# Attention scores in half legs: maxima turned per four heads and 256 queries, a score bank with two heads of one row half, lead of 14 maximum tiles

## The chip, the cores and the metric

The kernel is one launch on one core of a Trainium2 chip. The metric is the device time of that launch in microseconds (us). Five engines run their own instruction streams and meet at semaphores: PE (TensorE, the matmuls), DVE (VectorE), ACT (ScalarE), POOL (GpSimd) and SP (SyncE, which only issues DMAs here).

## The reference

Two transformer-like blocks run one after the other over 2 x 1024 tokens of 128 channels. The change touches only the attention of the first block:

```python
h = _layernorm(x, axis=-1) * (1 + ca) + sa
def _L0_attn_ref(x, Wq, Wk, Wv):
    H, hd = 16, 8
    q = (x @ Wq.T).reshape(N, S, H, hd).transpose(0, 2, 1, 3)
    k = (x @ Wk.T).reshape(N, S, H, hd).transpose(0, 2, 1, 3)
    v = (x @ Wv.T).reshape(N, S, H, hd).transpose(0, 2, 1, 3)
    energy = jnp.einsum('nhqd,nhkd->nhqk', q, k)
    attn = jax.nn.softmax(energy / jnp.sqrt(jnp.float32(hd)), axis=3)
    out = jnp.einsum('nhql,nhld->nhqd', attn, v)
    return out.transpose(0, 2, 1, 3).reshape(N, S, D)
x = x + ga * attention(h)
```

Behind it come the coupling network, two Mamba layers and a mixture of experts, all untouched by the change. With 2 sequences and 16 heads there are 32 heads, each with 1024 queries and 1024 keys.

## The kernel before, in words

**Tiling.** Queries and keys lie in bf16 rows, each number split into three bf16 parts, so that 48 rows (`KR`) carry the product of 8 channels, and 3 more rows (up to `KM` = 51) carry the negated maximum of each query. Of two neighbouring heads one lies in partitions 0 to 50, the other in 64 to 114 (`head_rows`: `64 * (j % 2)`), called row half 0 and row half 64 here. A *leg* is four heads and 512 queries; there are 16 legs. The heads of a leg are j = 0 to 3; j = 0 and 2 are in row half 0, j = 1 and 3 in row half 64.

**Three kinds of work.** (m) A *maximum tile* is 128 queries of one head against 1024 keys: two matmuls of 512 columns (`pe_max_score`, L548) into `max_ps`, which has room for two tiles, then one DVE reduction over 1024 columns (`ve_max_score`, L559). A leg has 16 tiles, the whole attention 256. When a leg's 16 tiles are reduced, POOL splits the maxima into three bf16 parts (`po_max_parts`, L568 to L574), PE turns them (`pe_max_turn`, L590), ACT copies them out (L596) and SP puts them into the query rows with four DMAs (`sp_max_turn`, L603). This is a *turn*. (s) A *score bank* is one matmul of 51 rows, 128 keys by 512 queries of one head (`pe_score`, L667), and one ACT exponential of 512 columns (`ac_exp`, L675). `HEADS` gives the order of the heads: (1, 3, 0, 2). A leg has 32 score banks. Three PSUM banks (`score_k`) go round (`score_bank`) among scores, turns and results: a new user waits for ACT to have read what was three users ago. (v) The product with the values is four matmuls of 256 columns over all 128 partitions (`pe_av`, L694), two for each group of four score banks; each shows in the profile as two records.

**Order.** The order is written out by hand. `ahead(v)` puts the first `AHEAD` = 22 maximum tiles ahead of all scores; the turn of leg 0 stands behind the tile `NU + 2` = 18. Then come 65 rounds of four tiles, eight score banks and four v each, by the strings in `ROUNDS`:

```python
ROUNDS = ("msmsvmsmsvvmsmsvmsms", "msmsmsmsvmsmsvvmsmsv", "msmsvmsmsvmsmsvmsmsv", "msmsvmsmsvmsmsvmsmsv")
return ((0, 2, 1, 3)[k // 4], k % 4) if leg == 0 else (k // 8 * 2 + k % 2, k % 8 // 2)
HEADS = (1, 3, 0, 2)
s, row = head_rows(leg, HEADS[r % 4])
```

Each `m` is one of a tile's two matmuls, so `msms` is one tile and two score banks; I call it a *slot*. PE takes its stream in this order. By `tile_of` the tiles alternate between row half 0 and row half 64 from slot to slot, and by `HEADS` the score banks are two of half 64 and then two of half 0. The strings have `v` behind most slots, and once in a leg three slots follow each other with no `v` between (the end of place 0 and the start of place 1). The turn of the next leg stands at the end of place 2, the loads of later heads (`sp_load`) behind it on SP. When the tiles are through, the last 22 slots have scores and values alone; DVE then does the first steps of the next stage (`ve_first_batch`).

Of the kernel before, what the change touches and what calls it, by code (L numbers as in the profile page):

```python
# [22 lines left out]
P = 128  # L23
# [5 lines left out]
TB = S // P  # L29
# [117 lines left out]
class Kernel:  # L147
# [282 lines left out]
    def attention(self):  # L430
        nc, A, pe, ve, ac, po, sp = self.nc, self.A, self.pe, self.ve, self.ac, self.po, self.sp
        with ExitStack() as scope:
# [16 lines left out]
            nr = sb("neg_max_rest", [P, 4, 4])  # L449
            ms = [sb(f"neg_max_parts{s}", [P, 4, 3, 4], BF16) for s in range(2)]  # L450
            mt = [sb(f"neg_max_rows{s}", [48, P], BF16) for s in range(2)]
# [69 lines left out]
            NLEG, NU, AHEAD = BH // 2, 16, 22  # L521
# [11 lines left out]
            def tile_of(leg, k):  # L533


                return ((0, 2, 1, 3)[k // 4], k % 4) if leg == 0 else (k // 8 * 2 + k % 2, k % 8 // 2)

            def pe_max_score(leg, k, half):
                t = NU * leg + k
                j, qt = tile_of(leg, k)  # L540
                s, row = head_rows(leg, j)
                if half == 0:
                    if t == 0:
                        pe.wait_ge(*first_half.at())
                    elif k == (0 if leg else 8):
                        pe.wait_ge(*loaded_at[leg // 2])
                    wait_from(pe, max_read.sem, t - 1)
# [5 lines left out]
            def ve_max_score(leg, k):  # L553
                j, qt = tile_of(leg, k)
                bank = (NU * leg + k) % 2 * 2
                if k == 0:
                    wait_from(ve, split.sem, 4 * (leg - 1))
                ve.wait_ge(*max_mm.at())
                ve.tensor_reduce(nm[leg % 2][:, 4 * j + qt:4 * j + qt + 1],  # L559
# [3 lines left out]
            def po_max_parts(leg):  # L563

                z, o = nm[leg % 2][:].rearrange("p (h k) -> p h k", h=4), ms[leg % 2]
                po.wait_ge(*max_read.at())
                wait_from(po, max_turned.sem, leg - 1)
# [8 lines left out]
            def max_score(v):  # L576

                leg, k, half = v // 2 // NU, v // 2 % NU, v % 2
                if leg >= NLEG:
                    return  # L580
                pe_max_score(leg, k, half)
                if half:
                    ve_max_score(leg, k)
                    if k == NU - 1:
                        po_max_parts(leg)

            def pe_max_turn(leg, bank, free):
                pe.wait_ge(split.sem, 4 * leg + 4)
                wait_from(pe, *free)
                pe.transpose(eps[:, bank, 0:64].bitcast(BF16)[0:3 * NU, :],  # L590
                             ms[leg % 2][:].rearrange("p h a k -> p (h a k)"), self.identb[:]).then_inc(*max_turned.up())

            def ac_max_turn(leg, bank):
                ac.wait_ge(max_turned.sem, leg + 1)
                wait_from(ac, max_in[leg % 2].sem, 64 * (leg // 2))
                ac.activation(mt[leg % 2][:], eps[:, bank, 0:64].bitcast(BF16)[0:3 * NU, :], ACT.Copy).then_inc(  # L596
                    *turn_read.up())

            def sp_max_turn(leg):
                sp.wait_ge(turn_read.sem, leg + 1)  # L600
                for j in range(4):
                    s, row = head_rows(leg, j)
                    sp.dma_start(qp[row + KR:row + KM, s, leg % 2, :].rearrange("a (k q) -> a k q", k=4),  # L603
                                 mt[leg % 2][12 * j:12 * j + 12, :]).then_inc(*max_in[leg % 2].up(16))
# [28 lines left out]
            def max_turn(leg):  # L633

                bank, free = score_bank()
                pe_max_turn(leg, bank, free)
                ac_max_turn(leg, bank)
                sp_max_turn(leg)
# [19 lines left out]
            HEADS = (1, 3, 0, 2)  # L658

            def pe_score(leg, r, bank, free):  # L660
# [2435 lines left out]
```

## Time and profile before

| what | us |
|---|---|
| median of 3 runs | 1158.91 |
| the three runs | 1160.96, 1148.05, 1158.91 |
| the profiled execution's own time | 1150.8 |
| its span, first to last instruction | 1149.3 |
| attention in it, to PE's first matmul of the next stage (L397) | 378.71 |

All sums below are made in the profiled execution, whose own time is 1.5 us over its span. It is not the middle of the runs: the median is 8 us longer. PE is the busiest engine by the page (90% of the span), DVE the next (84%).

### The profile page before, as it was taken

To read this page: it belongs to the slowest core of one execution; us is meant where nothing else is said; L and a number is where in the kernel's file an instruction comes from. 1 tells how busy PE (TensorE), PEld (TensorE's weight loads), DVE (VectorE), ACT (ScalarE), POOL (GpSimd) and SP (SyncE) were. 2 spreads that over 40 slices of the span, in tenths; PEclk is the share of its full clock that TensorE was granted. 3 is DMA by queue.
4 is the path that set the end of the run, shared out by engine and by line. 5 is a ranking of instruction groups with operands and counts; after the bars stand their busy time and mean duration, and the time that the engine had idled before them with its cause. 6 is when DMAs were issued, how large, how long until landed. Compare 5 with 4: busy or idle time off the path is not lost. (4 is left out here: it accounts for less than half of the span.)

```text
span 1149.3 us, 21244 instructions
## 1 busy us (share of the span) xinstructions
PE 1036.9 (90%) x7771; PEld 648.5 (56%) x7771; DVE 968.1 (84%) x1309; ACT 814.9 (71%) x1621; POOL 520.9 (45%) x487
## 2 busy tenths in 40 slices
PE   6899999999999887889999999899999984699992
PEld 4222222222222334458998984468888964488992
DVE  6899999999995676979999996989999996767774
ACT  3279898999998644978888844888888922265561
POOL 5400431010101211027899991048999972256663
PEclk9779999999999988799999999899999995699996
DMA  5210100001000420107999980118999967311124
GB/s 158 69 43 15 30 16 21 25 16 30 15 2 2 130 56 2 58 2 178 244 248 224 223 205 3 58 43 193 234 242 224 242 144 253 41 43 41 43 48 121
DMA packets 58374, 114.40 MB, mean 100 GB/s; under 512 B 15406, under 2 KB 28718, under 8 KB 58272
## 3 DMA queue, kind: packets, MB, share of 16 engines
q0 software_dynamic: 14880, 50.23, 22.2%
q1 hardware_dynamic: 40152, 60.62, 16.8%
q10 hardware_dynamic: 3240, 2.20, 0.7%
q8 instruction: 62, 1.02, 0.4%
q14 instruction: 40, 0.33, 0.1%
HBM read 55.47 MB, written 9.13 MB: 56 GB/s over the span
## 5 line engine op out<-in xcount | busy, mean ns | idle before, releaser
L2245 PEld LDWEIGHTS m_pair<-filter_w,delta_x_t 128*128 128x128 f32 x2560 | 294.0, 192 | 43.1 <-issue 43.1
L559 DVE TENSOR_REDUCE neg_max<-max_ps 128x1 f32<-128x1024 f32 x256 | 295.6, 1214 | 15.2 <-PE max_ps L548 15.0
L2245 PE MATMUL m_pair<-filter_w,delta_x_t 128*128 128x112 f32 (+3 forms) x2560 | 298.5, 276 | 9.8 <-DVE h_t L2272 3.3
L675 ACT ACTIVATE exp_scores<-score_k 128x512 f32<-128x512 f32 x512 | 270.8, 605 | 28.4 <-PE score_k L667 22.7
L2221 ACT ACTIVATE decay<-delta,a_log 128x1024 f32<-128x1024 f32 x128 | 145.7, 1142 | 49.7 <-DVE normed L2272 29.7
L548 PE MATMUL max_ps<-k_rows,q_rows 48*128 48x512 bf16 x512 | 163.0, 400 | 12.4 <-DVE neg_max L559 10.7
L2213 ACT ACTIVATE filter_w<-filter,b_t 128x112 f32<-128x112 f32 (+1 forms) x576 | 167.4, 374 | 0.0
L667 PE MATMUL score_k<-q_rows,k_rows 51*128 51x512 bf16 x512 | 163.0, 389 | 2.4 <-ACT exp_scores L675 0.6
L694 PE MATMUL av_ps<-exp_scores,v_cols 128*32 128x256 f32 x2048 | 158.2, 394 | 0.0
L568 POOL CAST neg_max_parts<-neg_max 128x16 bf16<-128x16 f32 x16 | 3.2, 197 | 235.0 <-DVE neg_max L559 235.0
L694 PEld LDWEIGHTS av_ps<-exp_scores,v_cols 128*32 128x32 f32 x2048 | 44.2, 109 | 92.0 <-ACT exp_scores L675 52.8
L548 PEld LDWEIGHTS max_ps<-k_rows,q_rows 48*128 48x128 bf16 x512 | 29.4, 95 | 116.4 <-DVE neg_max L559 75.0
L2263 DVE TENSOR_TENSOR_SCAN m_pair<-decay,m_pair 128x1024 f32<-128x1024 f32 x38 | 87.0, 2289 | 1.6 <-PE m_pair L2245 1.2
L2310 POOL TENSOR_TENSOR h_t<-h_t,c_row 128x1024 f32<-128x1024 f32 x30 | 81.6, 2718 | 13.0 <-DVE h_t L2272 13.0
L2310 POOL TENSOR_TENSOR normed<-normed,c_row 128x1024 f32<-128x1024 f32 x28 | 76.0, 2714 | 23.4 <-DVE normed L2272 23.4
L2907 PE MATMUL gate_up_ps<-tile_t,gate_up 128*128 128x128 f32 x624 | 77.6, 278 | 3.0 <-DVE tile_t L2889 2.0
L2272 DVE TENSOR_TENSOR_SCAN normed<-decay,m_pair 128x1024 f32<-128x1024 f32 x32 | 73.0, 2280 | 8.7 <-PE m_pair L2245 8.7
L2272 DVE TENSOR_TENSOR_SCAN h_t<-decay,m_pair 128x1024 f32<-128x1024 f32 x32 | 73.0, 2280 | 6.0 <-PE m_pair L2245 6.0
L2907 PEld LDWEIGHTS gate_up_ps<-tile_t,gate_up 128*128 128x128 f32 x624 | 72.7, 192 | 6.8 <-DVE tile_t L2889 6.8
L2358 PE MATMUL m_pair<-delta_x,ident 128*128 128x512 f32 x136 | 68.3, 598 | 0.0
L2920 ACT ACTIVATE silu_gate<-gate 128x512 f32<-128x512 f32 x39 | 24.6, 630 | 46.9 <-DVE gate L2915 46.9
L2946 POOL DMA_INDIRECT moe_out_rows<-tile_out,row_to x39 | 38.9, 996 | 38.6 <-ACT tile_out L2941 37.7
(335 smaller groups left out, 1631.4 us busy)
## 6 DMA issues: line engine op xcount, KB each, us to landing
c_row<-c_rows SPq DMA_DIRECT2D x64, 512.0 KB, 6.0
x_inner<-normed POOLq DMA_DIRECT2D x16, 512.0 KB, 6.5
delta_x<-mod_memory POOLq DMA_DIRECT2D x15, 512.0 KB, 8.1
delta_x<-x_inner POOLq DMA_DIRECT2D x15, 512.0 KB, 8.3
x_inner<-h_t POOLq DMA_DIRECT2D x14, 512.0 KB, 5.7
mod_memory<-h_t POOLq DMA_DIRECT2D x14, 512.0 KB, 9.2
mod_memory<-normed POOLq DMA_DIRECT2D x12, 512.0 KB, 8.8
gate_up_all<-in_gate_up_w SPq DMA_DIRECT2D x8, 512.0 KB, 7.3
```

The source lines that it names most:

```text
L548: mm = pe.matmul(mps[:, t % 2 * 2 + half, :], qp[row:row + KR, s, leg % 2, qt * P:(qt + 1) * P], kp[row:row + KR, s, half * CH:(half + 1) ...
L559: ve.tensor_reduce(nm[leg % 2][:, 4 * j + qt:4 * j + qt + 1], mps[:, bank:bank + 2, :].rearrange("p a q -> p (a q)"), AX_X, ALU.max, negat ...
L667: pe.matmul(eps[:, bank, :], kp[row:row + KM, s, kt * P:(kt + 1) * P], qp[row:row + KM, s, leg % 2, :], start=True, stop=True).then_inc(*s ...
L675: ac.activation(pt[a % 4][:, HEADS[r % 4], :], eps[:, bank, :], ACT.Exp, scale=SC).then_inc(*exped.up())
L694: mm = pe.matmul(avp[32 * j:32 * j + 32, qs], va[quad % 2][:, j, kt, :], pt[a % 4][:, j, qs], start=(kt == half == 0), stop=(kt == TB - 1) ...
L2213: w = ac.activation(wf[g % 3][:, lo:c * STEP + P], tri[min(c, 1)][:], ACT.Copy, scale=self.bT[b][:, c, n:n + 1])
L2221: ac.activation(da[u % 4], delta[:, blk, b, :], ACT.Exp, scale=am[:, l, blk, n:n + 1]).then_inc(*decay.up())
L2245: mm = pe.matmul(vps[blk][:, lo:hi], self.duT[b][:, c, blk * P:(blk + 1) * P], wf[g % 3][:, lo:hi], start=True, stop=True)
L2263: ve.tensor_tensor_scan(to, da[u % 4], vps[0][:], 0.0, ALU.mult, ALU.add).then_inc(*hs.up())
L2272: ve.tensor_tensor_scan(hh[g % 4], da[u % 4], vps[1][:], 0.0, ALU.mult, ALU.add).then_inc(*hs.up())
L2310: po.tensor_tensor(yacc[b][1] if n == 1 else hh[g % 4], hh[g % 4], csb[g % 3][:], ALU.mult).then_inc(*yg.up())
L2907: mm = pe.matmul(gups[j % 2][:, half, f * P:(f + 1) * P], gu[j % 3][:, half * FF + f * P:half * FF + (f + 1) * P], xt[j % 2][:], start=Tru ...
```

## The change

A turn now covers four heads and 256 queries (8 tiles, `NU` = 8), so there are 32 turns (`NTURN`) in place of 16, each with half the data: 24 rows in place of 48, DMAs of half the size. A score bank now holds two heads of 256 queries, both of one row half: two matmuls of 256 columns in place of one of 512. The exponential still takes 512 columns. `HEADS` is indexed by `r % 2`: banks alternate between half 64 (heads 1, 3) and half 0 (heads 0, 2). `ROUNDS` is as it was, and so is the alternation of the tiles' halves from slot to slot. `AHEAD` is 14. The turn of turn 0 stands behind tile 10, those that follow at the end of places 0 and 2. The memsets `po_ones(2, NS)` on POOL move from behind the projections to behind the split of turn 0, and SP's first loads wait for them. `ve_first_batch` takes two steps where it took one.

```diff
-            NLEG, NU, AHEAD = BH // 2, 16, 22
+            NLEG, NU, AHEAD = BH // 2, 8, 14
+            NTURN, HQ = 2 * NLEG, CH // 2
-                return ((0, 2, 1, 3)[k // 4], k % 4) if leg == 0 else (k // 8 * 2 + k % 2, k % 8 // 2)
+                j, q = ((0, 2, 1, 3)[k // 2], k % 2) if turn == 0 else (k // 4 * 2 + k % 2, k % 4 // 2)
+                return j, turn % 2 * 2 + q
...
-            HEADS = (1, 3, 0, 2)
+            HEADS = ((1, 3), (0, 2))
-                kt = r // 4
-                s, row = head_rows(leg, HEADS[r % 4])
+                leg, q0, kt = turn // 2, turn % 2 * HQ, r // 2
                 if r == 0:
-                    pe.wait_ge(max_in[leg % 2].sem, 64 * (leg // 2 + 1))
+                    pe.wait_ge(max_in[turn % 2].sem, 64 * (turn // 2 + 1))
                 wait_from(pe, *free)
-                pe.matmul(eps[:, bank, :], kp[row:row + KM, s, kt * P:(kt + 1) * P], qp[row:row + KM, s, leg % 2, :],
-                          start=True, stop=True).then_inc(*score_mm.up())
+                for c, j in enumerate(HEADS[r % 2]):
+                    s, row = head_rows(leg, j)
+                    mm = pe.matmul(eps[:, bank, c * HQ:(c + 1) * HQ], kp[row:row + KM, s, kt * P:(kt + 1) * P],
+                                   qp[row:row + KM, s, leg % 2, q0:q0 + HQ], start=True, stop=True)
+                mm.then_inc(*score_mm.up())
...
-                pe.wait_ge(exped.sem, 4 * a + 4)
+                pe.wait_ge(exped.sem, 4 * a + kt % 2 * 2 + 2)
...
                     max_turn(0)
+                    po.wait_ge(*split.at())
+                    po_ones(2, NS)
+                    sp.wait_ge(*rows_set.at())
                     for half in range(2):
                         sp_load(1, half)
...
-                po.wait_ge(*part_lo.at())
-                po_ones(2, NS)
-                sp.wait_ge(*rows_set.at())
...
                         if v % 2 == 0:
-                            ve_first_batch(v // 2 - NLEG * NU - 1)
+                            for step in range(2):
+                                ve_first_batch(v - 2 * NTURN * NU - 2 + step)
...
+                if place % 2 == 0 and n // 2 + 1 < NTURN:
+                    max_turn(n // 2 + 1)
                 if place == 2 and leg + 1 < NLEG:
-                    max_turn(leg + 1)
```

On PE in the middle of the attention, a slot with its v and the start of the next slot stood so before (`max_ps` is the tile, `score_k` the score bank, `av_ps` the product with the values):

```order
L548 MATMUL max_ps<-k_rows,q_rows 128x512
L667 MATMUL score_k<-q_rows,k_rows 128x512
L548 MATMUL max_ps<-k_rows,q_rows 128x512
L667 MATMUL score_k<-q_rows,k_rows 128x512
L694 MATMUL av_ps<-exp_scores,v_cols 32x256 x4
L548 MATMUL max_ps<-k_rows,q_rows 128x512
L667 MATMUL score_k<-q_rows,k_rows 128x512
```

and it stands so now:

```order
L550 MATMUL max_ps<-k_rows,q_rows 128x512
L673 MATMUL score_k<-q_rows,k_rows 128x256 x2
L550 MATMUL max_ps<-k_rows,q_rows 128x512
L673 MATMUL score_k<-q_rows,k_rows 128x256 x2
L702 MATMUL av_ps<-exp_scores,v_cols 32x256 x4
L550 MATMUL max_ps<-k_rows,q_rows 128x512
L673 MATMUL score_k<-q_rows,k_rows 128x256 x2
```

The order of kinds is the same; what changed is that each score bank is two matmuls, and the row half in which each bank lies.

The second place is PE at the end of place 0, inside the run of three slots without v. Nothing stood between the slots before; now the turn of a half leg does (L593 is `pe_max_turn`):

```order
L702 MATMUL av_ps<-exp_scores,v_cols 32x256 x4
L550 MATMUL max_ps<-k_rows,q_rows 128x512
L673 MATMUL score_k<-q_rows,k_rows 128x256 x2
L550 MATMUL max_ps<-k_rows,q_rows 128x512
L673 MATMUL score_k<-q_rows,k_rows 128x256 x2
L593 MATMUL score_k<-identb,neg_max_parts 24x128
L550 MATMUL max_ps<-k_rows,q_rows 128x512
L673 MATMUL score_k<-q_rows,k_rows 128x256 x2
L550 MATMUL max_ps<-k_rows,q_rows 128x512
```

So each leg has one more transpose on PE, which takes a score bank of its own.

The third place is POOL at the start, from the last split of the projections on. Before, the memset of the key rows came ahead of the first split of maxima:

```order
L788 TENSOR_TENSOR part<-part_rest,part 128x512 x4
L467 MEMSET k_rows 32x4096 x2
L568 CAST neg_max_parts<-neg_max 128x4x4
L570 TENSOR_TENSOR neg_max_rest<-neg_max,neg_max_parts 128x16
L572 CAST neg_max_parts<-neg_max_rest 128x4x4
L574 TENSOR_TENSOR neg_max_parts<-neg_max_rest,neg_max_parts 128x4x4
L655 COPY v_cols<-v_tok 128x8x8 x4
```

Now it stands behind it:

```order
L800 TENSOR_TENSOR part<-part_rest,part 128x512 x4
L571 CAST neg_max_parts<-neg_max 128x4x2
L573 TENSOR_TENSOR neg_max_rest<-neg_max,neg_max_parts 128x8
L575 CAST neg_max_parts<-neg_max_rest 128x4x2
L577 TENSOR_TENSOR neg_max_parts<-neg_max_rest,neg_max_parts 128x4x2
L467 MEMSET k_rows 32x4096 x2
L660 COPY v_cols<-v_tok 128x8x8 x4
```

The split of turn 0 has moved ahead of the memset, and the copy of the first values stays behind it.

## Rows read from the trace of the kernel before

**Rows 1.** Groups of the page: line engine op, busy us, mean ns, idle before

```profile
L559 DVE TENSOR_REDUCE neg_max<-max_ps 128x1 f32<-128x1024 f32 x256 | 295.6, 1214 | 15.2 <-PE max_ps L548 15.0
L675 ACT ACTIVATE exp_scores<-score_k 128x512 f32<-128x512 f32 x512 | 270.8, 605 | 28.4 <-PE score_k L667 22.7
L667 PE MATMUL score_k<-q_rows,k_rows 51*128 51x512 bf16 x512 | 163.0, 389 | 2.4 <-ACT exp_scores L675 0.6
```

**Rows 2.** Windows: PE, PEld, DVE, ACT, POOL busy (count), PEclk, DMA share, GB/s

```profile
66.00:70.00 4.00, 3.82 (x24) 0.66 (x24) 3.25 (x4) 2.93 (x6) 0.00 (x0) 0.50 0.13 42
...
240.00:300.00 60.00, 58.95 (x615) 17.33 (x617) 57.12 (x54) 55.38 (x109) 5.15 (x23) 1.00 0.09 25
```

**Rows 3.** Timeline of PE, two slots and a turn: start us, us, instruction

```profile
212.07 0.39 PE L548 MATMUL max_ps<-k_rows,q_rows 48*128 48x512 bf16 x1
212.07 0.39 PE L667 MATMUL score_k<-q_rows,k_rows 51*128 51x512 bf16 x1
212.30 0.38 PE L548 MATMUL max_ps<-k_rows,q_rows 48*128 48x512 bf16 x1
...
212.61 0.64 PE L694 MATMUL av_ps<-exp_scores,v_cols 128*32 128x256 f32 x8
213.18 0.39 PE L548 MATMUL max_ps<-k_rows,q_rows 48*128 48x512 bf16 x1
...
215.39 0.24 PE L590 MATMUL score_k<-identb,neg_max_parts 128*48 128x128 bf16 x1
215.56 0.39 PE L548 MATMUL max_ps<-k_rows,q_rows 48*128 48x512 bf16 x1
```

**Rows 4.** Timeline of PE: ends of one leg, and the run of three slots

```profile
205.18 0.39 PE L548 MATMUL max_ps<-k_rows,q_rows 48*128 48x512 bf16 x1 [0.21 <-DVE neg_max L559]
...
223.82 0.39 PE L548 MATMUL max_ps<-k_rows,q_rows 48*128 48x512 bf16 x1
...
224.63 0.39 PE L548 MATMUL max_ps<-k_rows,q_rows 48*128 48x512 bf16 x1 [0.21 <-DVE neg_max L559]
...
226.62 0.64 PE L694 MATMUL av_ps<-exp_scores,v_cols 128*32 128x256 f32 x8
```

**Rows 5.** Timeline of PE: matmuls of one row half behind each other

```profile
38.28 1.03 PE L548 MATMUL max_ps<-k_rows,q_rows 48*128 48x512 bf16 x4
...
352.93 0.60 PE L667 MATMUL score_k<-q_rows,k_rows 51*128 51x512 bf16 x2
353.46 0.64 PE L694 MATMUL av_ps<-exp_scores,v_cols 128*32 128x256 f32 x8
```

**Rows 6.** Timeline: weight loads between f32 matmuls of 512 columns, and 16 of 128

```profile
16.40 0.19 PEld L764 LDWEIGHTS score_k<-h_t,w_qkv 128*128 128x128 f32 x1 [0.24 <-issue]
16.83 0.19 PEld L764 LDWEIGHTS score_k<-h_t,w_qkv 128*128 128x128 f32 x1 [0.24 <-issue]
...
36.40 1.95 PE L801 MATMUL score_k<-w_qkv,h_t 128*128 128x128 f32 x16
```

**Rows 7.** Timeline of the lead: reductions, memset, first turn, first score

```profile
38.92 22.39 DVE L559 TENSOR_REDUCE neg_max<-max_ps 128x1 f32<-128x1024 f32 x19 [0.42 <-PE max_ps L548]
...
40.96 7.06 POOL L467 MEMSET k_rows<- 32x4096 bf16 x2
...
54.28 0.20 POOL L568 CAST neg_max_parts<-neg_max 128x16 bf16<-128x16 f32 x1 [6.25 <-DVE neg_max L559]
...
57.11 3.14 SPq L603 DMA_DIRECT2D q_rows<-neg_max_rows  x4
...
61.36 0.60 PE L667 MATMUL score_k<-q_rows,k_rows 51*128 51x512 bf16 x1 [0.58 <-DMA q_rows<-neg_max_rows]
```

**Rows 8.** Timeline of the slots without tiles, to the next stage

```profile
349.38 0.60 PE L667 MATMUL score_k<-q_rows,k_rows 51*128 51x512 bf16 x2
...
368.75 8.63 ACT L675 ACTIVATE exp_scores<-score_k 128x512 f32<-128x512 f32 x16
...
378.71 0.42 PEld L397 LDWEIGHTS max_ps<-ident,normed 128*128 128x128 f32 x4 [0.41 <-issue]
```

More of the change, by code:

```diff
@@ L531, in head_rows, with tile_of, pe_max_score @@
                 return 2 * (leg // 2 % 3) + j // 2, 64 * (j % 2)
-            def tile_of(leg, k):
-                return ((0, 2, 1, 3)[k // 4], k % 4) if leg == 0 else (k // 8 * 2 + k % 2, k % 8 // 2)
-            def pe_max_score(leg, k, half):
-                t = NU * leg + k
-                j, qt = tile_of(leg, k)
+            def tile_of(turn, k):
+                j, q = ((0, 2, 1, 3)[k // 2], k % 2) if turn == 0 else (k // 4 * 2 + k % 2, k % 4 // 2)
+                return j, turn % 2 * 2 + q
+            def pe_max_score(turn, k, half):
+                t, leg = NU * turn + k, turn // 2
+                j, qt = tile_of(turn, k)
                 s, row = head_rows(leg, j)
@@ L544, in pe_max_score @@
                         pe.wait_ge(*first_half.at())
-                    elif k == (0 if leg else 8):
+                    elif k == (0 if turn else 4) and turn % 2 == 0:
                         pe.wait_ge(*loaded_at[leg // 2])
@@ L576, in max_score @@
             def max_score(v):
-                leg, k, half = v // 2 // NU, v // 2 % NU, v % 2
-                if leg >= NLEG:
+                turn, k, half = v // 2 // NU, v // 2 % NU, v % 2
+                if turn >= NTURN:
                     return
-                pe_max_score(leg, k, half)
+                pe_max_score(turn, k, half)
                 if half:
-                    ve_max_score(leg, k)
+                    ve_max_score(turn, k)
                     if k == NU - 1:
-                        po_max_parts(leg)
@@ L587, in pe_max_turn @@
-            def pe_max_turn(leg, bank, free):
-                pe.wait_ge(split.sem, 4 * leg + 4)
+                        po_max_parts(turn)
+            def pe_max_turn(turn, bank, free):
+                pe.wait_ge(split.sem, 4 * turn + 4)
                 wait_from(pe, *free)
                 pe.transpose(eps[:, bank, 0:64].bitcast(BF16)[0:3 * NU, :],
[L591 to L596, printed above, removed]
+                             ms[turn % 2][:].rearrange("p h a k -> p (h a k)"), self.identb[:]).then_inc(
+                                 *max_turned.up())
@@ L597, in ac_max_turn, with sp_max_turn @@
+            def ac_max_turn(turn, bank):
+                ac.wait_ge(max_turned.sem, turn + 1)
+                wait_from(ac, max_in[turn % 2].sem, 64 * (turn // 2))
+                ac.activation(mt[turn % 2][:], eps[:, bank, 0:64].bitcast(BF16)[0:3 * NU, :], ACT.Copy).then_inc(
                     *turn_read.up())
-            def sp_max_turn(leg):
-                sp.wait_ge(turn_read.sem, leg + 1)
+            def sp_max_turn(turn):
+                leg, q0 = turn // 2, turn % 2 * HQ
+                sp.wait_ge(turn_read.sem, turn + 1)
@@ L601, in sp_max_turn @@
                 for j in range(4):
                     s, row = head_rows(leg, j)
-                    sp.dma_start(qp[row + KR:row + KM, s, leg % 2, :].rearrange("a (k q) -> a k q", k=4),
-                                 mt[leg % 2][12 * j:12 * j + 12, :]).then_inc(*max_in[leg % 2].up(16))
+                    sp.dma_start(qp[row + KR:row + KM, s, leg % 2, q0:q0 + HQ].rearrange("a (k q) -> a k q", k=2),
+                                 mt[turn % 2][6 * j:6 * j + 6, :]).then_inc(*max_in[turn % 2].up(16))
@@ L631, in po_divide, with max_turn @@
                     rc[leg % 2][:][:, :, :, None].to_broadcast([P, 4, 4, HD]), ALU.mult).then_inc(*divided.up())
-            def max_turn(leg):
+            def max_turn(turn):
                 bank, free = score_bank()
-                pe_max_turn(leg, bank, free)
-                ac_max_turn(leg, bank)
-                sp_max_turn(leg)
+                pe_max_turn(turn, bank, free)
+                ac_max_turn(turn, bank)
+                sp_max_turn(turn)
                 read.append(turn_read.at())
```

55 lines of the change are left out of this document (29 added, 26 removed).

## Prediction, made before the changed kernel was run

> **What bounds the kernel now.** I read the page's groups first. In the attention three engines carry nearly the same load: 256 reductions on DVE, 512 exponentials on ACT, and on PE the tiles, scores and values [rows 1]. The windows then say who is full: in 240 to 300 us PE is busy 58.95 of 60 us and DVE 57.12, with the PE clock at its full level of 2.4 GHz [rows 2]. So neither has room. The timeline of PE tells why it gets through at all. In a slot the tile's matmul and the score matmul start in the same hundredth (212.07 both), the second pair 0.23 us later, the v 0.54 us after the start, and the next slot 1.11 us after it (213.18) [rows 3]. Two matmuls of 512 columns, one per row half, run side by side in the time of one.
>
> The other half of this reading is what happens in one row half. The four matmuls at 38.28 are two tiles of one half, and nothing else is on PE: 1.03 us for four, less the 0.39 that the last takes from start to end, is 0.64 / 3 = 0.21 us from start to start [rows 3, 5]. And in the slots without tiles two score matmuls, both of one half, take 0.53 us up to the v (352.93 to 353.46), as long as four take where they go in pairs across the halves (0.54) [rows 3, 5]. So a matmul of 512 columns costs 0.21 us, in a pair across the halves nothing more, and a second one in the same half another 0.21.
>
> A leg takes 224.63 - 205.18 = 19.45 us, 1.22 per slot [rows 4]. Most of it is PE without a gap. The exception is the run of three slots without v: from 223.82 to the v at 226.62 it takes 2.80 us where PE has 3 x 0.44 + 0.1 = 1.4 us of work; the rest is waiting for DVE and for score banks [rows 4]. So PE's work in a leg is about 19.45 - 1.4 = 18.05 us, and the slack that a costlier slot may use is 1.4 us a leg, 0.09 us a slot.
>
> **The change part by part.**
>
> *The lead.* Scores now start behind 14 tiles instead of 22. The reductions go at 22.39 / 19 = 1.18 us each; the first of that row is tile 3, so tile 7 ends at 38.92 + 5 x 1.18 = 44.8 [rows 7]. In the old kernel tile 15 ended at 54.2 and POOL's split began at 54.28; the first score came at 61.36, 7.1 us later, having waited for the DMAs issued from 57.11 [rows 7]. The PE position of the turn is two tiles further on in both. 44.8 + 7.1 = 51.9; since the tile that PE had to pass there (tile 18, now 10) keeps the same distance, I take 51.5 for the first score. Gain 9.9 us. POOL's memset (7.06 us) moves behind the split, ends at about 46 + 7.1 = 53.1, and hides behind the first round; the values' copy behind it is wanted only by the first v, a round later. SP's 18 loads wait for it and are wanted by tile 32, about 25 us later. Cost 0, at most 1.5 us if the DMAs of turn 1, queued behind those loads on SP, come late.
>
> *The slots, on PE.* This is the large term. By `tile_of` and `HEADS` the halves in a slot were 0, 64, 0, 64 and in the next 64, 0, 64, 0: each tile matmul met a score of the other half. Now the banks alternate 64, 0 in every slot, and the tiles still change only from slot to slot. An even slot reads m0, s64 s64, m0, s0 s0: the first bank runs beside the first m, but the second bank is of the same half as both m, and stands behind them. An odd slot reads m64, s64 s64, m64, s0 s0: here the first bank is in line and the last one runs beside the second m. Row half 0 (or 64) gets three units of 512 columns in a slot where it got two, and the v needs all 128 partitions, so nothing slips past it. The slot grows by one unit: 0.21 us. In a leg 16 x 0.21 = 3.4 us.
>
> *Splitting a score matmul.* Two matmuls of 256 columns with a weight load each replace one of 512. No bf16 matmul of 256 columns on row halves is in the trace. Lower end 0: the columns are the same. The nearest row is f32: 16 matmuls of 128 columns with a load each take 1.95 us, (1.95 - 0.28) / 15 = 0.111 each with about 0.28 for the last one, where those of 512 columns stand 16.83 - 16.40 = 0.43 apart, a quarter of which is 0.108 [rows 6]. So a piece that streams for 0.11 us hides its load but for 0.004 us; two more per slot are 0.01, 0.1 us a leg. Upper end: a load that isn't hidden. The loads between the f32 matmuls last 0.19 us [rows 6]; a bf16 load should be half of it, say 0.1, on each of two pieces, 0.2 us a slot. I take 0.01, the nearest row.
>
> The Trainium skill, TensorEngine Tiling (Array Packing), section Instruction Overhead, gives each matmul about 60 cycles of overhead; that would be 25 ns for each of two more per slot, some 12 us over 242 slots, as an estimate from that page. The f32 row above shows 4 ns where a load goes with each piece, and I keep to the row.
>
> *Turns.* 16 more transposes on PE: from the turn at 215.39 to the next matmul are 0.17 us [rows 3]. One is added a leg, and it stands inside the run of three slots, where it takes a score bank. With three banks the last score of the run has to wait until ACT has gone through four exponentials and the copy; exponentials follow each other at 8.63 / 16 = 0.54 us [rows 8]. PE needs 3 x 0.64 + 0.17 = 2.1 us for the run, ACT lets it through in about 2.5, and DVE's next reduction asks about the same. So 0.17 + 0.4 us a leg. DVE, POOL, ACT and SP have the rest of the turns beside PE's work: with PE the bound, DVE drops to 1.2 of 1.4 us a slot. Bounds: 0 and 1 us a leg.
>
> *A leg after:* 18.05 + 3.4 + 0.1 + 0.6 = 22.15; the waits for banks that one sees here and there in the old leg are in the 18.05. I add 0.15 for more of them and take 22.3, 1.39 us a slot, against 19.45.
>
> *The clock.* In 66 to 70 us the granted clock is 0.50, that is 1.2 GHz, after a lead in which PE mostly waited for DVE, and PE is full [rows 2]. From the first score (61.36) to the first slot without tiles (349.38) are 288.0 us, and 234 slots at 19.45 / 16 would be 284.5 [rows 4, 7, 8]: the slow start costs 3.5 us. It will come again; PE has more to do in it, so I take 4.5.
>
> *The last slots.* From 349.38 to 378.71 are 29.3 us for 22 slots and the last values [rows 8]. Eight slots go, at about 1.1 us (two exponentials at 0.54): 20.5 us stay. The second bank of a slot now runs beside the first one's second matmul, which PE can use and ACT can't. DVE's steps, taken in pairs, have 14 slots for what had 22: cost 0 to 2 us, I take 0.
>
> *Sum.* 51.5 + 242 x 22.3 / 16 (337.3) + 4.5 + 20.5 = 413.8 us for PE's first matmul of the next stage, where it was 378.7: 35 us later. What follows isn't touched. 1150.8 + 35 = 1186 in the profiled execution's terms. The runs of before have their median at 1158.9, 8 us above it, which would make 1194; the middle of the four times is 1155, and so I say 1188.
>
> **The rivals.**
>
> *The halves don't matter* (faster). If PE fits the scores in wherever a half is free, a slot costs what it did, and the lead's gain stays: 51.5 + 15.1 x (19.45 + 0.3) + 3.5 + 20.5 = 374, 5 us less, 1150 against my 1155 of before; with the run of three absorbing the turn too, 9 less, 1146. By the spread of the runs a part of this would be measured as over 1%. For it: the row tiles are independent, and PE's slack is small but real. Against it: 0.53 us for two of one half against 0.54 for four in pairs [rows 3, 5]. It decides if the slot stays under 1.25 us.
>
> *Half of it shows* (no change). If only one kind of slot, even or odd, is longer (the trailing bank of a slot running on beside the next slot's start where no v stands between, or being hidden by v's weight loads), a leg is 18.05 + 1.7 + 0.7 = 20.5, then 51.5 + 310 + 4.5 + 20.5 = 386.5, 8 us more: 1163. Against it: 14 of 16 slots have a v behind them.
>
> *The turns come late* (slower still). A turn's four DMAs took 61.36 - 57.11 = 4.3 us from the first issue to the score that waited for them [rows 7], some 5 us with the transpose and the copy ahead of them, and the scores of a turn stand 4 slots, 5.5 us, behind the transpose. Now it runs 32 times, with loads in the same SP queue every second time. If each is 0.7 us late, 31 x 0.7 = 22 us come on top: 1210.
>
> *Every piece pays its load* (slower still): 0.2 us a slot more, 242 x 0.2 = 48 us: 1236.
>
> **How the numbers follow.** Forecast 0.69; halves don't matter 0.09; half of it 0.08; turns late 0.09; loads shown 0.05. A measurement of this kernel can tell about 1% from no change. Faster by over 1% is a bit over half of the first rival: 0.05. Within 1% are the rest of it and the second: 0.12. Slower: 0.83. The range leaves out the first two rivals' faster ends and the last: 1160 to 1220.
>
> **What would show it right or wrong.** In the timeline of PE, from one slot's first m to the next one's with a v between: 1.32 us (before 1.11), and the v 0.75 us after the slot's start. In an even slot the first score piece starts with the m, and the second bank's pieces only 0.2 us after the second m; in an odd slot the other way round. A leg of 22.3 us. DVE's reductions wait for L550 some 50 us in all where they waited 15.0 [rows 1]; the exponentials wait as much. The first score at 51.5, L397 at about 414. If the slot is 1.11, the term of the halves is wrong; if 1.5, the loads; if it is 1.32 and the end later than 420, look for waits of the score matmuls for the DMAs of q_rows.

## The result, and the profile after

The changed kernel takes 1212.53 us (median of 6 runs, 1205.59 to 1239.63), the kernel before 1155.82 us (median of 6). The ratio is 1.049, with a 95% interval from 1.042 to 1.057: slower by 57 us. The forecast was 1188 us, slower, and the time lies inside the stated range; but it named only one of the two causes of the loss, and priced the other at nothing. Ratios here and below leave out runs more than 1.5% above the fastest of their kernel. The profiled execution took 1215.62 us with a span of 1214.3 us, 65 us more than the span of before, and 63.8 us of it lie in the attention: PE's first matmul of the next stage stands at 442.49 us where it stood at 378.71 [rows 8].

The timeline of PE in the changed kernel, an even slot, an odd slot and the start of the next one (start us, us, instruction), answers to [rows 3]:

```profile
287.31 0.39 PE L550 MATMUL max_ps<-k_rows,q_rows 48*128 48x512 bf16 x1
287.31 0.39 PE L673 MATMUL score_k<-q_rows,k_rows 51*128 51x256 bf16 x2
287.53 0.38 PE L550 MATMUL max_ps<-k_rows,q_rows 48*128 48x512 bf16 x1
287.75 0.38 PE L673 MATMUL score_k<-q_rows,k_rows 51*128 51x256 bf16 x2
288.06 0.64 PE L702 MATMUL av_ps<-exp_scores,v_cols 128*32 128x256 f32 x8
288.63 0.39 PE L550 MATMUL max_ps<-k_rows,q_rows 48*128 48x512 bf16 x1
288.64 0.59 PE L673 MATMUL score_k<-q_rows,k_rows 51*128 51x256 bf16 x4
289.08 0.38 PE L550 MATMUL max_ps<-k_rows,q_rows 48*128 48x512 bf16 x1
289.38 1.07 PE L702 MATMUL av_ps<-exp_scores,v_cols 128*32 128x256 f32 x16
```

The slot is 288.63 - 287.31 = 1.32 us where it was 1.11, and the v stands 0.75 us behind the slot's start where it stood 0.54. In the even slot the second bank starts 0.22 us behind the second m; in the odd slot the second m starts 0.45 us behind the first, because the first bank is in its way. The code puts the second bank of an even slot and the first bank of an odd one into the row half of the slot's tile, and these are the places where the starts stand apart; two matmuls of one row half go one behind the other.

The windows of the changed kernel (PE, PEld, DVE, ACT, POOL busy with counts, then PEclk) show something that before doesn't have:

```profile
60.00:120.00 60.00, 59.80 (x617) 21.86 (x614) 50.09 (x45) 47.78 (x93) 9.52 (x31) 0.97 0.07 19
120.00:180.00 60.00, 57.05 (x446) 18.70 (x442) 38.78 (x44) 36.53 (x70) 13.18 (x33) 0.72 0.04 12
180.00:240.00 60.00, 57.10 (x450) 18.89 (x446) 38.58 (x44) 36.33 (x70) 12.18 (x32) 0.72 0.05 14
240.00:300.00 60.00, 59.71 (x627) 22.23 (x619) 51.52 (x46) 49.65 (x99) 5.43 (x26) 1.00 0.08 22
```

A mean of 0.72 in a window of 60 us means that 60 x (1 - 0.72) / 0.5 = 33.6 us of it ran at the level of 1.2 GHz. This happens twice, in the middle of the attention, and in those windows the trace has 446 and 450 matmul records of PE where it has 617 and 627 in the others. Before, the clock was at its full level from about 70 us to 364 us, in the slots without tiles.

What stands ahead of the first such stretch is in the timeline of POOL and PE around 125 us:

```profile
115.64 1.70 POOL L315 TENSOR_SCALAR mod_memory<-mod_memory 128x256 f32<-128x256 f32 x2
...
125.94 0.72 POOL L286 TENSOR_TENSOR mod_memory<-gate_tmp 128x256 f32<-128x256 f32 x1
126.61 0.19 POOL L571 CAST neg_max_parts<-neg_max 128x8 bf16<-128x8 f32 x1
...
127.42 0.20 POOL L577 TENSOR_TENSOR neg_max_parts<-neg_max_rest,neg_max_parts 128x8 bf16<-128x8 f32 x1
127.67 0.23 PE L593 MATMUL score_k<-identb,neg_max_parts 128*24 128x128 bf16 x1 [2.85 <-POOL neg_max_parts L577]
...
189.35 0.23 PE L593 MATMUL score_k<-identb,neg_max_parts 128*24 128x128 bf16 x1 [2.81 <-POOL neg_max_parts L577]
```

Twice in the attention POOL finishes the gate rows of a layer (`po_finish_rows`, L315 and L278 to L286) in one block, here from 115.64 to 126.66. The split of the next turn is queued behind it. With a turn every 16 slots that block had room: before, POOL had been idle for 5.41 us when the next maxima came. With one every 8 slots the last of the maxima is reduced by 123.0 us, 3.6 us before POOL is free. PE reaches the transpose, waits 2.85 us, and from 128 to 162 us runs at half clock. The second layer's block does the same: 2.81 us, and half clock from 190 to 224 us. So the time of the attention adds up as

- first score at 51.69 (61.36 before [rows 7]),
- 242 slots at 22.17 / 16 us: 335.3 (22.17 from the turns at 225.94 and 292.46 us, three legs apart),
- the two waits and the half clock behind them: between the turns at 114.14 and 304.03 us lie 7 legs, which is 155.2 at full pace and took 189.9, so 34.7,
- 19.0 from the first slot without a tile (423.49) to the end (442.49),
- and 1.8, which is what is left of the 442.49, for the start at half clock.

DVE's reductions now wait 77.4 us for the tile matmuls in place of 15.0, the exponentials 80.9 us for the scores in place of 22.7 [rows 1]. The forecast had some 50 us for each, in a kernel without the 34.7 us above:

```profile
L561 DVE TENSOR_REDUCE neg_max<-max_ps 128x1 f32<-128x1024 f32 x256 | 305.0, 1218 | 79.2 <-PE max_ps L550 77.4
L682 ACT ACTIVATE exp_scores<-score_k 128x512 f32<-128x512 f32 x512 | 277.7, 596 | 86.0 <-PE score_k L673 80.9
```

### The profile page after: what moved, and what is told of

Its sections match the earlier page's. It is cut to its first block and busy times, and to the rows that moved or that the text cites. A ratio compares the mean times of both kernels' runs of the same rounds, so it can differ in the third digit from the quotient of the medians.

```text
span 1214.3 us, 22520 instructions
## 1 busy us (share of the span) xinstructions
PE 1106.7 (91%) x8299; PEld 697.7 (57%) x8299; DVE 981.2 (81%) x1309; ACT 823.2 (68%) x1637; POOL 534.6 (44%) x551
## 5 line engine op out<-in xcount | busy, mean ns | idle before, releaser
L561 DVE TENSOR_REDUCE neg_max<-max_ps 128x1 f32<-128x1024 f32 x256 | 305.0, 1218 | 79.2 <-PE max_ps L550 77.4
L682 ACT ACTIVATE exp_scores<-score_k 128x512 f32<-128x512 f32 x512 | 277.7, 596 | 86.0 <-PE score_k L673 80.9
L550 PE MATMUL max_ps<-k_rows,q_rows 48*128 48x512 bf16 x512 | 192.1, 420 | 3.5 <-DVE neg_max L561 2.9
L673 PE MATMUL score_k<-q_rows,k_rows 51*128 51x256 bf16 x1024 | 184.2, 291 | 2.4 <-ACT exp_scores L682 0.5
L702 PE MATMUL av_ps<-exp_scores,v_cols 128*32 128x256 f32 x2048 | 171.7, 423 | 0.0
L571 POOL CAST neg_max_parts<-neg_max 128x8 bf16<-128x8 f32 x32 | 6.1, 190 | 281.6 <-DVE neg_max L561 281.6
L550 PEld LDWEIGHTS max_ps<-k_rows,q_rows 48*128 48x128 bf16 x512 | 40.0, 96 | 109.5 <-issue 78.5
L673 PEld LDWEIGHTS score_k<-q_rows,k_rows 51*128 51x128 bf16 x1024 | 66.0, 98 | 63.3 <-ACT exp_scores L682 19.4
```

The costliest lines, as they stand in the source:

```text
L550: mm = pe.matmul(mps[:, t % 2 * 2 + half, :], qp[row:row + KR, s, leg % 2, qt * P:(qt + 1) * P], kp[row:row + KR, s, half * CH:(half + 1) ...
L561: ve.tensor_reduce(nm[turn // 2 % 2][:, 4 * j + qt:4 * j + qt + 1], mps[:, bank:bank + 2, :].rearrange("p a q -> p (a q)"), AX_X, ALU.max, ...
L673: mm = pe.matmul(eps[:, bank, c * HQ:(c + 1) * HQ], kp[row:row + KM, s, kt * P:(kt + 1) * P], qp[row:row + KM, s, leg % 2, q0:q0 + HQ], st ...
L682: ac.activation(pt[a % 4][:, r % 4, :], eps[:, bank, :], ACT.Exp, scale=SC).then_inc(*exped.up())
L702: mm = pe.matmul(avp[32 * j:32 * j + 32, qs], va[quad % 2][:, j, kt, :], pt[a % 4][:, r, c * HQ:(c + 1) * HQ], start=(kt == turn % 2 == 0) ...
```

## The experiments

**e1: only the alternating halves, in the kernel before.**

```diff
-            HEADS = (1, 3, 0, 2)
+            HEADS = (1, 0, 3, 2)
```

> The kernel before with one line changed: HEADS = (1, 0, 3, 2), so that the score banks alternate between row half 64 and 0 in every slot, as in the changed kernel; lead of 22 tiles, 16 turns, scores in one matmul of 512 columns. If the row halves are the cause of the longer slot, PE's slot goes from 1.11 to 1.32 us here too and a leg from 19.45 to about 21.7 us, 14.6 legs make 33 us, and the time is about 1150 + 32 = 1183 in a profile whose clock stays as in before, ratio 1.028. If the pieces of 256 columns or the additional turns are the cause, this kernel takes what before takes, ratio 1.00. If long full load on PE is what makes the clock fall, the granted clock falls to 0.5 in the attention here too; if POOL's late split is, it does not.

Measured: ratio 1.040 (1.032 to 1.047), 1195.99 us against 1149.33. The slot on PE in this kernel:

```profile
121.48 0.39 PE L548 MATMUL max_ps<-k_rows,q_rows 48*128 48x512 bf16 x1
...
122.23 0.64 PE L694 MATMUL av_ps<-exp_scores,v_cols 128*32 128x256 f32 x8
122.80 0.39 PE L548 MATMUL max_ps<-k_rows,q_rows 48*128 48x512 bf16 x1
```

It is 1.32 us, v at 0.75, with the long lead, 16 turns and undivided scores. A leg takes 22.27 us (turns at 298.34 and 320.61), about as long as the 22.17 of the changed kernel, which has one more turn in it. So one line makes the longer slot, and the pieces and the turns have no part in it. The clock is at its full level from 120 us to the end of the attention with PE busy 58.34 of 60 us, so a long full load did not take it away here. What I had not expected is the start: the half clock from the lead lasts until 111 us, as two windows of 20 us show:

```profile
80.00:100.00 20.00, 20.00 (x109) 4.30 (x105) 10.37 (x9) 9.64 (x18) 0.84 (x4) 0.50 0.07 22
100.00:120.00 20.00, 19.55 (x137) 5.06 (x129) 12.92 (x13) 12.88 (x25) 1.17 (x5) 0.72 0.00 1
```

Its four runs take 1188.5 and 1188.6 us at a mean clock of 0.94, and 1203.3 and 1204.8 at 0.928. The trace is of the longest of the four. In it PE's first matmul of the next stage stands at 433.54 us, 54.8 later than before, and that divides: 234 slots with a tile at 22.27 in place of 19.45 us a leg are 41.2, the end without tiles is 2.8 shorter, the first score 0.3 later, and the half clock in the slots with tiles costs 19.7 where it cost 3.5. So the halves at full clock are 38.7 us. The shorter two runs are 39 us above before; no trace shows whether their half clock ended earlier, but their mean clock fits that.

**e2: only the divided scores, in the kernel before.**

```diff
-                pe.matmul(eps[:, bank, :], ..., qp[row:row + KM, s, leg % 2, :], ...).then_inc(*score_mm.up())
+                for c in range(2):
+                    cols = slice(c * 256, (c + 1) * 256)
+                    mm = pe.matmul(eps[:, bank, cols], ..., qp[row:row + KM, s, leg % 2, cols], ...)
+                mm.then_inc(*score_mm.up())
```

> The kernel before with each score matmul of 512 columns issued as two of 256 columns of the same head, nothing else. If a piece hides its weight load, as the f32 row said, the slot on PE stays 1.11 to 1.13 us and the time within 0.5% of before. If each piece pays 0.1 us for its load, the slot is 1.3 us and the time about 1180. If the overhead of some 60 cycles a matmul holds, the slot is 1.16 us, and with 0.09 us of slack a slot nearly all of it is absorbed: under 1%.

Measured: ratio 1.006 (1.002 to 1.010), over 10 runs. Two starts of slots in its timeline:

```profile
212.53 0.39 PE L548 MATMUL max_ps<-k_rows,q_rows 48*128 48x512 bf16 x1
212.53 0.39 PE L669 MATMUL score_k<-q_rows,k_rows 51*128 51x256 bf16 x2
...
213.64 0.39 PE L548 MATMUL max_ps<-k_rows,q_rows 48*128 48x512 bf16 x1
```

The slot is 1.11 us, to the hundredth what it was. Pieces of 256 columns hide their weight loads, and the rule of 60 cycles a matmul (the Trainium skill, TensorEngine Tiling (Array Packing), Instruction Overhead), which would make it 1.16, isn't seen in this slot, where the matmuls of the other half run beside them. The half per cent isn't in the slots with tiles; in the profiled run it lies behind them. There a stretch at half clock lasts from 365 to 389 us, where before had one from 364 to 367, and PE's first matmul of the next stage comes at 389.99 us, 11.3 later. In these slots both score banks are of one row half and stand behind each other, in this kernel as in before. Its runs spread from 1149.5 at a mean clock of 0.942 to 1165.2 at 0.923, so I don't put it down to the edit for certain.

**e3: POOL's block in two halves, in the changed kernel.** `po_finish_rows` takes a list of parts and is called with one part in each of four legs:

```diff
-                    if leg in (2, 4):
-                        self.po_finish_rows(leg // 2 - 1, rows_in[leg // 2 - 1])
-                        if leg == 2:
+                    if leg in (2, 3, 4, 5):
+                        self.po_finish_rows(leg // 2 - 1, rows_in[leg // 2 - 1], (leg % 2,))
+                        if leg == 3:
                             m_row0 = self.gate_rows.at()
```

> The changed kernel with POOL's 10 us of gate rows (po_finish_rows) called in two halves, of 5 us each, in rounds a leg apart, for both layers; all else as it is. If that block of work on POOL delays the split of the next turn, so that PE waits 2.8 us at L593 and then runs at half clock for 34 us, twice, then both waits and both stretches of half clock go, and the profile is about 31 to 36 us shorter: 1180 to 1185, ratio to before 1.025. If PE's clock falls for being full without a pause, the stretches stay or come elsewhere, and only the two waits go: 1209, ratio 1.045.

Measured: 1187.66 us against 1149.33, ratio 1.039 (1.031 to 1.046); three of its four runs lie at 1186.4 to 1188.0, the fourth at 1202.4 with a mean clock of 0.925. Against the changed kernel's 1.049 this is a gain of some 12 us by the two ratios, whose intervals overlap, and of 28 us between the profiled executions (1215.62 and 1187.33). No transpose waits for POOL by more than 0.3 us, and the two stretches of 34 us are gone:

```profile
120.00:180.00 60.00, 58.48 (x585) 21.66 (x582) 50.16 (x53) 46.97 (x93) 16.17 (x39) 0.94 0.06 17
180.00:240.00 60.00, 58.49 (x622) 21.62 (x615) 52.62 (x56) 48.32 (x96) 12.04 (x40) 1.00 0.07 22
```

One stretch of 7 us is left in the first window, from 147.6 us, behind the first of two waits for DVE. The second wait is as long, and no half clock follows it:

```profile
145.78 0.37 PE L550 MATMUL max_ps<-k_rows,q_rows 48*128 48x512 bf16 x1 [1.32 <-DVE neg_max L561]
...
193.97 0.37 PE L550 MATMUL max_ps<-k_rows,q_rows 48*128 48x512 bf16 x1 [1.32 <-DVE neg_max L561]
```

PE reaches the next stage at 413.66 us. The forecast had 413.8, without POOL.

**e4: the halves matched, in the changed kernel.** The first two banks of each four are of half 64 for two key tiles, the other two of half 0:

```diff
-                leg, q0, kt = turn // 2, turn % 2 * HQ, r // 2
+                leg, q0, kt = turn // 2, turn % 2 * HQ, r // 4 * 2 + r % 2
...
-                for c, j in enumerate(HEADS[r % 2]):
+                for c, j in enumerate(HEADS[r // 2 % 2]):
...
-                pe.wait_ge(exped.sem, 4 * a + kt % 2 * 2 + 2)
+                pe.wait_ge(exped.sem, 4 * a + 4)
-                    r, c = kt % 2 * 2 + 1 - j % 2, j // 2
+                    r, c = (1 - j % 2) * 2 + kt % 2, j // 2
```

> The changed kernel with the banks of a slot both in the half that the slot's tile does not use: two banks of heads 1 and 3 for two key tiles, then two of heads 0 and 2 (the values wait for all four banks). If the halves are the cause of the longer slot, the slot is 1.11 to 1.13 us again, a leg about 19.8 us. POOL's block of 10 us is now in front of a split that is due after 9.6 us, so its delay is larger, about 4 us, and the clock falls twice as before: about 1150 - 10 + 5 + 8 + 30 = 1180. If the halves are not the cause, the slot stays 1.32 us and the time 1212.

Measured: ratio 1.011 (1.007 to 1.016), 1166.01 us over 9 runs. The slot is 1.11 us again (243.99 to 245.10). The halves are the larger cause: by the ratios 44 of the 57 us go with this edit alone. In the profiled execution it is more, 56 of 64 us in the attention, and not all of that is the slot: a leg of 19.69 in place of 22.17 us is 37.5 over 242 slots, and most of the rest is half clock. POOL's block is in the way as foreseen, by more than in the changed kernel, since the slots are shorter:

```profile
121.25 0.23 PE L593 MATMUL score_k<-identb,neg_max_parts 128*24 128x128 bf16 x1 [3.98 <-POOL neg_max_parts L577]
...
168.21 0.28 PE L593 MATMUL score_k<-identb,neg_max_parts 128*24 128x128 bf16 x1 [4.40 <-POOL neg_max_parts L577]
```

But the half clock behind the waits is far shorter, and that is most of why the time is below the 1180 expected:

```profile
120.00:180.00 60.00, 52.64 (x563) 21.46 (x563) 46.18 (x51) 44.03 (x88) 15.92 (x40) 0.86 0.05 15
180.00:240.00 60.00, 57.51 (x690) 24.25 (x690) 56.89 (x62) 53.88 (x109) 7.20 (x34) 1.00 0.07 22
```

60 x 0.14 / 0.5 = 17 us for both waits together, where the changed kernel has 67 us behind two shorter waits. So the two causes are not independent: between e4 and e5, whose halves are both matched, the same block on POOL costs 6.9 us of the attention in the profiles (386.04 and 379.17) and 13 us by the ratios.

**e5: both mends** (the edits of e3 and e4 together).

> The changed kernel with both mends: banks in the row half that the tile of the slot does not use, and POOL's gate rows in two halves of 5 us. If the two causes are all there is, a slot is 1.11 us, no turn waits for POOL by more than 1 us, no stretch of half clock after the start, and the gain of the earlier start is kept: some 9 us under before less 0.3 us a leg for the additional turns, about 1144 in a profile, ratio 0.990 to 0.997. If POOL's spread work does not matter for the clock, it takes what e4 takes, ratio 1.011.

Measured: ratio 0.9997 (0.997 to 1.002), 1148.91 us over 12 runs against 1149.50. With both causes gone the kernel takes what the kernel before takes. The gain of the earlier start didn't come: the first score stands at 51.66 us, 9.7 earlier than before, and PE is at the next stage at 379.17, 0.5 later. A leg takes 19.69 us (transposes at 253.90 and 273.59) against 19.45, 3.6 us over 15.1 legs. And there are two waits of PE for DVE, each followed by a stretch of 6.8 us at half clock:

```profile
136.76 0.37 PE L550 MATMUL max_ps<-k_rows,q_rows 48*128 48x512 bf16 x1 [1.87 <-DVE neg_max L561]
...
180.12 0.37 PE L550 MATMUL max_ps<-k_rows,q_rows 48*128 48x512 bf16 x1 [1.88 <-DVE neg_max L561]
```

Ahead of each DVE clamps the gate columns (`ve_mod_gates`, from 132.87 and from 176.23 us). In before the same waits are there, at 143.57 and 183.75 us, but 1.16 us long, and the clock stays full.

**e6: e3 for the first layer's rows alone.**

> The changed kernel with POOL's gate rows spread for the first layer's rows only, the second layer's in one block as before. If each block costs its wait of 2.8 us and a stretch at half clock behind it, one such wait and one such stretch are left, the one near 190 us, and the time lies half way between the changed kernel and e3: about 1200. If it were the sum of POOL's work and not its block, it would be 1187 or 1212.

Measured: 1204.10 us, ratio 1.049 (1.043 to 1.055). One wait of 2.81 us is left, at 190.28, and a stretch of 48 us at half clock behind it; the other has gone, and 120 to 180 us have a clock of 1.00. By median it lies about half way as expected, but by ratio it takes what the changed kernel takes (1.049), so the time does not decide how the loss divides between the two blocks. The timeline does: each block has its own wait and stretch. The profile has a second difference, which also lengthens it: the half clock from the lead lasts to 102 us, where e3, with the same instructions up to there, was through at 62:

```profile
60.00:90.00 30.00, 30.00 (x185) 8.32 (x181) 14.95 (x13) 14.18 (x26) 0.78 (x4) 0.50 0.06 17
90.00:120.00 30.00, 30.00 (x266) 10.45 (x259) 21.60 (x20) 21.26 (x41) 3.46 (x17) 0.81 0.05 15
...
180.00:240.00 60.00, 57.20 (x386) 17.96 (x384) 34.15 (x39) 32.64 (x62) 11.87 (x27) 0.60 0.05 14
```

So how long the half clock lasts is not fixed by the kernel's instructions alone.

**e7: the long lead in the changed kernel** (`AHEAD = 22`, nothing else).

> The changed kernel with AHEAD = 22 in place of 14, nothing else. The first score comes 9.4 us later (8 reductions of 1.18 us), 8 slots are without a tile at 1.1 us instead of with one at 1.39, so it is 9.4 + 8.8 - 11.1 = 7 us longer if POOL's block delays the split as before. But the split is now due when eight more tiles are through ahead of PE's transpose, so the transpose comes some 10 us after it: POOL's delay is hidden, no wait at L593 and no half clock after the start: 1212 + 7 - 34 = 1185. If the time is 1219, POOL's delay is not what makes the clock fall.

Measured: 1217.28 us, ratio 1.059 (1.053 to 1.065). A miss of 32 us, though the part on POOL came as expected: no transpose waits for POOL. The stretch from the lead, however, now lasts till 138 us, with PE busy all the time:

```profile
60.00:120.00 60.00, 59.77 (x345) 18.10 (x345) 32.83 (x28) 31.66 (x58) 2.93 (x15) 0.50 0.03 8
120.00:180.00 60.00, 59.81 (x541) 20.44 (x539) 44.97 (x41) 43.05 (x85) 15.36 (x36) 0.85 0.06 17
```

All four runs have a mean clock of 0.912 to 0.917. POOL's wait is one way into half clock, the lead is another, and what costs is how long it stays.

**e8: e5 with DVE's clamps spread** (`ve_mod_gates` takes one gate at a time, in legs 3, 4, 5 and 6).

> The kernel of e5 with DVE's clamping of the gate columns (ve_mod_gates, two chains of five small operations, 2.7 us) called one chain at a time, in rounds a leg apart. In e5 PE waited 1.87 and 1.88 us for DVE behind these two blocks, and a stretch of 6.8 us at half clock followed each. If that wait is what takes the clock away, both waits shrink to 0.5 us and both stretches go: 2 x (1.4 + 3.4) = 9 us less, ratio to before about 0.992. If the stretches have another cause, the time stays, ratio 1.000.

Measured: ratio 0.998 (0.994 to 1.001), over 12 runs. The waits for DVE are now 0.88 us each and one of the two stretches at half clock is gone (180 to 240 us have 1.00, 120 to 180 still 0.94). The other begins at 136.3 us, behind a wait of 0.88 for DVE at 133.92 and one of 0.40 for POOL at 136.04; two more waits of 0.88, at 157.12 and 177.75, have full clock behind them. So the length of a single wait does not decide. As to the time, PE is at the next stage at 374.25 us, 4.5 earlier than before. In the total that can't be told from no change: even with both causes mended the half legs don't measurably beat the kernel before.

**e9: PE as the bound with matched halves, in the kernel before.** Each v is done twice, so that numerators and denominators both double:

```diff
                 for j in range(4):
+                    pe.matmul(avp[32 * j:32 * j + 32, qs], va[quad % 2][:, j, kt, :], pt[a % 4][:, j, qs],
+                              start=(kt == half == 0), stop=False, skip_group_check=True)
+                for j in range(4):
                     mm = pe.matmul(avp[32 * j:32 * j + 32, qs], va[quad % 2][:, j, kt, :], pt[a % 4][:, j, qs],
-                                   start=(kt == half == 0), stop=(kt == TB - 1), skip_group_check=True)
+                                   start=False, stop=(kt == TB - 1), skip_group_check=True)
```

> The kernel before with every product with the values done twice into the same sums (numerators and denominators double, so the quotient is the same). Row halves stay matched; PE's slot goes from 1.11 to about 1.54 us, above what DVE asks (1.18), so PE is the bound here as in the changed kernel, even more so. This asks what makes the half clock last: in before it ends 27 us after it began in the lead, in kernels with the alternating banks it lasted up to 96. If being the bound is enough, the stretch from the lead lasts 60 us or more here too and the mean clock is about 0.91 to 0.93, the time about 1270. If it takes the row halves in series, the stretch is about 27 us, and the time is 1150 + 15.1 x 5.6 + 9 = 1245.

Measured: 1262.05 us, ratio 1.085 (1.082 to 1.089), four runs within 2.5 us, mean clock 0.942 to 0.945, where before had 0.930 to 0.941 in this comparison. With before at 1163.9 in this comparison the difference is 98 us, near the 95 that the sum without a long stretch gave. The slot is 1.53 us (189.88 to 191.41), a leg 26.06 us (turns at 209.61 and 235.67), 6.6 more than before, which is 100 us over 15.1 legs. The clock is up again by 70 us:

```profile
60.00:120.00 60.00, 57.87 (x677) 20.15 (x679) 45.63 (x39) 41.79 (x80) 2.78 (x13) 0.92 0.10 28
120.00:180.00 60.00, 59.01 (x762) 22.17 (x758) 45.91 (x50) 42.02 (x81) 13.40 (x26) 1.00 0.06 15
```

So in this kernel PE was the bound, with a slot longer than the changed kernel's, and still left the half clock quickly. PE is busy 57.87 and 59.01 us of 60 here, somewhat less than the 59.80 of the changed kernel, and that difference is a rival that no run takes away. Of the kernels here only those with score and tile in one row half had stretches over 30 us in the attention; e2's 24 us in the slots without tiles, where score stands behind score in one half, is the next longest apart from the leads.

## Why the prediction was right or wrong

**Right: the slot.** "The slot grows by one unit: 0.21 us" is what the timeline shows (1.11 to 1.32), the v at 0.75 included; e1 shows that the order of the halves makes it by itself, and e4 that matching them takes it away. The leg was forecast at 22.3 us and is 22.17, but the working behind that number is only partly right. The forecast took off 1.4 us of slack from the run of three slots, and added 16 x 0.21 = 3.4 for the slots and 0.6 for the turn. What the timelines show is 13 slots outside that run at 0.21 more, 2.7 us, while the run hardly changes: 2.80 us before [rows 4], 2.89 in e1 (308.20 to 311.09) and 2.90 in the changed kernel with the turn inside it (291.71 to 294.61). The slack stayed in the run, took in the longer slots there and the turn, and the errors cancel. Where e5 has matched halves, the turns and all else that is new cost 0.24 us a leg.

**Right: splitting is free in the slot.** 0.01 us a slot was forecast, 0.00 measured (e2).

**Right: the lead, as far as it goes.** 51.5 us forecast for the first score, 51.69 measured; the slots without tiles took 19.0 us where 20.5 were forecast, and the start at half clock cost 1.8 where I took 4.5.

**Wrong: "DVE, POOL, ACT and SP have the rest of the turns beside PE's work".** This step set POOL's side of a turn at nothing, and it is the step that failed; it is why the forecast's 1186 us for the profiled execution fell 30 us short. It counted what a turn adds to POOL, and not what a turn waits for in POOL's queue. The block of gate rows is 11 us long here, the two turns that enclose it are due 10.7 us apart on PE (114.14 and 124.82), and so one split in each layer comes late by almost 3 us. The price is 34.7 us in the profiled execution, of which only 5.7 are the waits and 29 the two stretches of 34 us at half clock: at 2.40 us a slot (213.62 to 216.02) each stretch does 14.2 slots, which at full clock are 19.7 us. Removed (e3), PE is at the next stage at 413.66 us; forecast without it was 413.8. That the two agree to 0.1 us is luck: against the forecast e3 is 2.5 us shorter in first score, slots and end, and 2.4 longer in the rest, with a DVE wait and a stretch of half clock that were not foreseen. By medians the removal is worth about 25 us, by the ratios 12; stretches of half clock of other lengths in some runs of both are the likely reason for the spread, but only one run of each has a trace.

**Not foreseen: how long the half clock stays.** The forecast took the start's loss as a constant of some us. In the alternating order it was 1.8 us once (the changed kernel) and far more in e1 (19.7), e6 and e7. That it was small in the changed kernel's trace is luck: e6 has the same instructions up to 102 us and stayed at half clock until then.

**The hint for the case of a late end** ("look for waits of the score matmuls for the DMAs of q_rows") pointed at the wrong place: those waits are 0.2 us in all from 110 to 410 us. The rival of the late turns had the right object and the wrong link: a turn was late, but on POOL ahead of the transpose, in two legs and not in all. Its 1210 us is near the 1212.53 by chance.

The other rivals are out: the halves matter (e1, e4), both kinds of slots show it (287.31 to 288.63 even, 115.62 to 116.94 odd), and no piece pays its load (e2).

## What to carry to other kernels

Where matmuls of half the rows run in pairs, the order of the row halves is part of the schedule: a change of the grain of one stream (banks of two heads) has to be checked against the alternation of the other, slot by slot, and here one line of head order was worth 39 us at full clock, and 46 by the ratio of all runs (e1). When something is done twice as often, look in every queue that it passes for the longest block of other work, and compare that block with the new distance between two uses, not with the mean load. And a wait of TensorE is to be priced with the time at half clock behind it: behind the waits of 1.9 to 4.4 us this was 2 to 17 times the wait in these runs, and half of it was lost.

## What the runs showed that I had not expected

Once the scores had begun, the granted clock fell behind every wait of PE of 1.9 us (e5), 2.8 (the changed kernel, e6), 4.0 and 4.4 us (e4). Of the shorter waits for DVE, 0.88 to 1.32 us in before, e2, e3, e4, e6 and e8, two had half clock behind them, one of 1.32 in e3 and one of 0.88 in e8, and others of the same length had none. In the slots without tiles a wait of 0.59 us for ACT was followed by 3 us at half clock in before (361.48 us) and by 24 us in e2 (363.64 us). What followed was not in proportion to the wait: 6.8 us at half clock behind 1.9, 17 us in all behind 4.0 and 4.4 with matched halves; 34 and 34 us behind 2.85 and 2.81, and 48 behind 2.81, with alternating ones.

The stretch from the lead was back at full clock by 61 to 72 us in all kernels with matched halves (before, e2, e4, e5, e8 and e9). With the alternating order it lasted to 63 us (the changed kernel, e3), 102 (e6), 111 (e1) and 138 (e7), with PE busy by the page throughout. e9 speaks against PE's being the bound as the reason, though its PE is a little less full, and it ran on another chip than e1 and e7, one on which before takes 14 us more; that the series in one row half is the reason follows only from comparing these eleven kernels, and the changed kernel's and e3's own short leads speak against its being enough. What the chip counts, and why kernels that are equal up to that point (e3 and e6) leave half clock 39 us apart, stays open.
